# Routed expert tiles in pairs: the down product contracted as 128 rows plus two 48-row remainders

## The chip, the cores and the metric

The kernel runs on one core of one Trainium2 chip. The metric is the device time of one execution in microseconds. The time before is 397.71 us, the median of three runs (397.56 to 398.35).

## What is computed

An attention-like mixing step with a long convolution is followed by a mixture-of-experts feed-forward layer. Only the second part matters here:

```python
scores = softmax(xt @ Wg.T)                    # xt: 2048 tokens x 256, 16 experts
# 4 experts per token, out of the best 2 of 4 groups; combine holds their scores, else 0
h = silu(einsum('td,eid->eti', xt, W1)) * einsum('td,eid->eti', xt, W3)   # 176 wide
expert_out = einsum('eti,edi->etd', h, W2)
y = einsum('etd,te->td', expert_out, combine)
z = silu(xt @ Ws1.T) * (xt @ Ws3.T) @ Ws2.T    # shared experts, 352 wide
return x + y + z
```

The inner width of a routed expert, 176, is more than the 128 rows over which the array contracts in one pass.

## The kernel before

The first half of the span computes the mixing step, the router and the shared experts in 16 units of 128 tokens. Each token row is scattered to a scratch in HBM, sorted by expert, four copies of each. The **routed stage** then works through 72 tiles of 128 rows. A tile belongs to one expert; tiles 16 to 23 are **mixed**: their upper and lower 64 rows belong to two experts, and the second expert's weights ("others", 608 KB each) are loaded while tiles 5 to 14 run.

For each tile, in the order of its life:

- **gather** (SyncE, L357 to L368): one DMA of 144 KB from the scratch into one of four buffers `xg`. Gather t waits until `turn_x(t-4)` and `take(t-4)` have used that buffer. A mixed tile has two DMAs of 72 KB. The last 8 tiles go to buffers of their own (L410) and are gathered long before their use.
- **turn_x** (TensorE, L1395 to L1404): two transposes of the rows; ScalarE copies them to SBUF (`src_tr`, L547).
- **up** (TensorE, L1364 to L1385): 352 columns, contraction 256 in two matmuls. In a mixed tile each matmul is two, on the two column halves of the array (L1374 and L1377).
- **silu** (ScalarE, L553), **take** (VectorE, L1112 to L1126: the gate of each row, picked from the gathered row by the tile's expert) and **hidden** (VectorE, L1089: silu times gate times the second half of up).
- **turn_h** (TensorE, L1387 to L1393): two transposes of 88 of the 176 columns each; VectorE copies them (`copy_h`, L1096).
- **down** (TensorE, L1441 to L1459): 256 columns, contraction 88 twice (L1456), in a mixed tile on two column halves (L1448, L1451). ScalarE copies the result (`store_y`, L559).
- **place** (VectorE, L1131: the row numbers for the scatter; waits until the scatter of tile t-4 has landed) and **send** (GpSimd, L713 to L719: an indirect DMA of the tile's results to a second scratch).

Every engine's order is written out by hand. TensorE in step t: up(t), turn_x(t+1), down(t-2), turn_h(t-1). VectorE: take(t), hidden(t), copy_h(t-1), place(t). ScalarE: silu(t), src_tr(t+1), store_y(t-2). The two buffers of `up_ps`, `hid`, `ht_ps`, `hid_tr` and `dn_ps` alternate with the tile's parity.

From tile 32 on, in rounds of eight tiles, SyncE also **reads back** finished results (L392, 1024 KB for two units of tokens) and **stores** finished units (L395). In round m it issues gathers 8m to 8m+3, then the store, which waits on `finished`, then the read-back, then gathers 8m+4 to 8m+7, all on one queue. VectorE adds the read-back rows in four steps spread over the tiles of the round (L1199 to L1208); the last of them, in step j = 6, signals `finished`. The first read-back, in round 4, has no store before it. At the very start, tile 0 is turned, then `down_shared(14)` runs on TensorE, then step 0.

float32 matmuls leave two records in the trace, with a weight load each; transposes leave one.

## Time and profile before

| | |
|---|---|
| median of three runs | 397.71 us (397.56 to 398.35) |
| span of the profiled execution | 395.4 us |
| median less span | 2.3 us |
| routed stage, first up (tile 0) to last up (tile 71) | 198.60 to 382.44 us |
| TensorE busy over the span | 97% |
| mean granted TensorE clock | 0.998 |

The span runs from the first to the last instruction of the profiled execution. The profile is read per stage: a view of one stretch shows how much of it an engine was busy, and a view of instructions in order of time shows what each one waited for. Idle time of an engine that isn't the last one to be waited for costs nothing.

### The profile page before, as it was taken

Reading aid. Unit: us, or ns where it says so; the run is one execution under the profiler, and the core shown is the slowest. Engines: PE = TensorE matmul, PEld = TensorE weight load, DVE = VectorE, ACT = ScalarE, POOL = GpSimd, SP = SyncE. Lnnn points to the kernel's source line nnn. Section 1 sums busy time; section 2 is a strip of 40 time slices with the busy share of each in tenths; the row PEclk is TensorE's granted clock in tenths of the full one; section 3 lists DMA queues with packets and bytes.
Section 4 is the critical chain, followed back from the end, with each engine's and each line's share of the span. In section 5 each row is a group of like instructions: output and inputs, shape, how many; then the busy total and the mean of one; then the engine's idle time right before and its main releaser. Section 6 shows DMA issues by size and latency. Waiting matters only on the chain.

```text
span 395.4 us, 9070 instructions
## 1 busy us (share of the span) xinstructions
PE 384.7 (97%) x2146; PEld 279.3 (71%) x2147; DVE 244.1 (62%) x676; ACT 162.9 (41%) x494; POOL 180.3 (46%) x225
## 2 busy tenths in 40 slices
PE   6999999999999999999999999999999999999996
PEld 6788888888888546555667675446767777777765
DVE  3577577987988465788735344443445464646466
ACT  5347656564564362101124333333333333334431
POOL 3254323337888573565553333333333333334333
PEclk9999999999999999999999999999999999999999
DMA  7974474368879996256376873334474737362737
GB/s 248 363 254 139 163 277 144 133 206 278 309 250 335 414 419 258 96 207 223 104 215 219 321 239 107 87 95 134 127 246 136 242 115 242 115 232 103 264 97 251
DMA packets 37812, 83.09 MB, mean 210 GB/s; under 512 B 5930, under 2 KB 25870, under 8 KB 35728
## 3 DMA queue, kind: packets, MB, share of 16 engines
q1 hardware_dynamic: 31248, 64.83, 49.1%
q0 software_dynamic: 6528, 17.84, 11.6%
q8 instruction: 16, 0.26, 0.3%
q14 instruction: 20, 0.16, 0.1%
HBM read 60.21 MB, written 23.48 MB: 212 GB/s over the span
## 4 chain that ended last, share of the span: by engine, by line
PE 79%; DVE 10%; DMA 4%; issue 2%; ACT 2%; SPq 1%; DVEq 1%; POOL 0%; POOLq 0%
PE heads L1382 18%; PE bank L1456 13%; PE heads L1271 11%; PE heads L1424 7%; PE heads L1273 5%; PE bank L1437 5%; PE heads L1392 4%; PE bank L1403 4%; PE bank L1285 3%; DVE kv L734 3%; PE heads L1374 3%; DMA toep<-toep_in 2%; PE bank L1448 2%; DVE prod L763 2%; DMA y_scratch<-toep,dest_i 2%
## 5 line engine op out<-in xcount | busy, mean ns | idle before, releaser
L716 POOL DMA_INDIRECT y_scratch<-toep,dest_i x72 | 71.8, 997 | 112.0 <-DVE dest_i L1131 96.0
L1382 PE MATMUL heads<-experts,toep 128*128 x256 | 86.6, 461 | 0.6 <-DVE toep L1089 0.5
L1271 PE MATMUL heads<-toep,kv 128*128 128x256 f32 x256 | 77.9, 386 | 1.9 <-DVE kv L734 0.8
L661 POOL DMA_INDIRECT rows_scratch<-rows,slot_i x64 | 63.3, 989 | 35.4 <-issue 19.5
L1456 PE MATMUL bank<-experts,toep 88*128 x256 | 66.2, 381 | 1.6 <-DVE toep L1096 1.6
L553 ACT ACTIVATE toep<-heads 128x176 f32<-128x176 f32 x72 | 22.8, 317 | 78.1 <-PE heads L1382 67.2
L1382 PEld LDWEIGHTS heads<-experts,toep 128*128 128x128 f32 x256 | 43.7, 190 | 14.8 <-issue 1.1
L1273 PEld LDWEIGHTS heads<-toep,kv 128*128 128x128 f32 x256 | 48.7, 190 | 6.5
L763 DVE TENSOR_TENSOR prod<-heads,ctx_rep 128x1024 f32<-128x1024 f32 x32 | 39.1, 1221 | 22.3 <-PE bank L1285 19.9
L1096 DVE COPY toep<-heads 88x256 f32<-88x256 f32 x72 | 30.2, 419 | 31.1 <-PE heads L1392 31.1
L1273 PE MATMUL heads<-toep,kv 128*128 128x128 f32 x256 | 49.2, 274 | 0.0
L1456 PEld LDWEIGHTS bank<-experts,toep 88*128 88x128 f32 x256 | 43.7, 190 | 6.1 <-issue 2.3
L559 ACT ACTIVATE toep<-bank 128x256 f32<-128x256 f32 x72 | 27.6, 383 | 39.5 <-PE bank L1456 34.1
L1424 PE MATMUL heads<-xn_tr_all,ws 128*128 128x512 f32 (+1 forms) x96 | 43.5, 596 | 0.0
L1089 DVE SCALAR_TENSOR_TENSOR toep<-toep,heads 128x176 f32<-128x176 f32 x72 | 28.6, 398 | 23.2 <-ACT toep L553 18.1
L1271 PEld LDWEIGHTS heads<-toep,kv 128*128 128x128 f32 x256 | 38.8, 192 | 2.6 <-issue 1.4
L734 DVE TENSOR_TENSOR kv<-bank,ctx_tr 128x2048 f32<-128x2048 f32 x15 | 34.2, 2282 | 0.1
L1403 PEld LDWEIGHTS bank<-ident,toep 128*128 128x128 f32 x128 | 17.3, 141 | 18.8 <-issue 12.4
L1424 PEld LDWEIGHTS heads<-xn_tr_all,ws 128*128 128x128 f32 (+1 forms) x96 | 16.9, 181 | 19.0 <-issue 18.4
L547 ACT ACTIVATE toep<-bank 128x256 f32<-128x256 f32 x72 | 27.5, 382 | 5.7 <-PE bank L1403 5.5
L1392 PE MATMUL heads<-ident,toep 128*88 128x128 f32 x144 | 27.8, 275 | 0.0
L1126 DVE COPY toep<-toep 128x2 f32 x56 | 10.1, 180 | 24.1 <-issue 15.1
(240 smaller groups left out, 513.4 us busy)
## 6 DMA issues: line engine op xcount, KB each, us to landing
ctx_rep<-ctxr_in SPq DMA_DIRECT2D x16, 1024.0 KB, 5.0
experts<-experts_in SPq DMA_DIRECT2D x16, 608.0 KB
toep<-rows_scratch SPq DMA_DIRECT2D x56, 144.0 KB
prod<-y_scratch SPq DMA_DIRECT2D x5, 1024.0 KB, 5.5
rows_scratch<-pad_row SPq DMA_DIRECT2D x17, 144.0 KB, 1.8
ctx_tr<-ctxt_in SPq DMA_DIRECT2D x16, 128.0 KB
toep<-toep_in SPq DMA_DIRECT2D x4, 512.0 KB, 7.0
ctx_n<-ctx_in SPq DMA_DIRECT2D x16, 128.0 KB, 2.1
```

Of the source, the lines that this page charges most:

```text
L661: pool.indirect_dma_start(rows_d, bass.IndirectOffsetOnAxis(ap=slot_i[:, u, k:k + 1].bitcast(U32), axis=0), rows[:, u, :], None).then_inc( ...
L716: pool.indirect_dma_start(y_d, bass.IndirectOffsetOnAxis(ap=dest_i[b][:, 0:1].bitcast(U32), axis=0), y_sb[b], None, bounds_check=TOPK * TO ...
L734: nc.vector.tensor_tensor(kv[:, u % 2, :, :].rearrange("p b (g i j) -> p (b g) i j", i=C, j=C), tr_ps.rearrange("p b (g i) -> p (b g) i", ...
L763: nc.vector.tensor_tensor(prod[:, par, :, :], y_ps[par], ctx_rep[:, u % 2, par::2, :], ALU.mult).then_inc(prod_ready, 1)
L1096: nc.vector.tensor_copy(hid_tr[p], ht_ps[p]).then_inc(htr_ready, 1)
L1271: nc.tensor.matmul(y_ps[par][:, i, :], kv[:, q, 0, h * P:(h + 1) * P], toep[:, q * HH + h, :], start=True, stop=False)
L1273: last = nc.tensor.matmul(y_ps[par][:, i, P:], kv[:, q, 1, h * P:(h + 1) * P], toep[:, q * HH + h, 0:P], start=False, stop=True)
L1382: last = nc.tensor.matmul(up_ps[p], x_tr[p][:, blk, :], up_w(e, blk), start=blk == 0, stop=blk == LB - 1)
L1392: last = nc.tensor.transpose(ht_ps[p][:, c, :], hid[p][:, c * HI:(c + 1) * HI], ident[:])
L1403: last = nc.tensor.transpose(xt_ps[p][:, blk, :], src[:, blk * P:(blk + 1) * P], ident[:])
L1424: last = nc.tensor.matmul(bank[2 * (s % 2) + w][0:rows_c, :].rearrange("p (u n) -> p u n", u=GT), ws13[:, blk, w, c0:c0 + rows_c], xn_tr_a ...
L1456: last = nc.tensor.matmul(dn_ps[p], hid_tr[p][:, c, :], down_w(e, c), start=c == 0, stop=c == 1)
```

## The change

Tiles t and t+1 (t even) go as a pair. The 176 inner columns are split as 128 and 48 in place of 88 and 88.

- TensorE's step for a pair: up(t), up(t+1), turn_x(t+2), turn_x(t+3), down of the pair before, turn_h of this pair. turn_h has three transposes for both tiles: the 128 columns of each, and one block that holds both remainders (48 columns of t at 0, 48 of t+1 at 64).
- down has four products for both tiles: first the two 48-row remainders, one on partitions 0 to 47, one on 64 to 111, each into its own PSUM bank, then the two 128-row products that add to them. In mixed tiles the remainders are four, on the four quarters of the array, and the 128-row products lie on column halves.
- VectorE's step: take(t), hidden(t), take(t+1), hidden(t+1) in two instructions (48 and 128 columns), a copy of the second tile's 48 rows of W2 to the partitions from 64 on (two such copies for a mixed pair), one copy_h of 384 columns for the pair, place(t), place(t+1).
- ScalarE's step: silu twice, src_tr twice, store_y twice.
- `hid`, `ht_ps` and `hid_tr` have one buffer in place of two. The gathers, their four buffers, the loads of the others, the stores and read-backs are issued by the same code as before.
- The four adding steps of a round stand after the pairs j = 2 (step 0), j = 4 (steps 1 and 2) and j = 6 (step 3).
- Before tile 0's up, both tile 0 and tile 1 are turned.

The core of the diff:

```diff
+            def routed_pair(t, b, before):            # ScalarE
+                silu(t, 0)
+                silu(t + 1, 1)
+                if not (isinstance(t, int) and t == LIVE - 2):
+                    src_tr(t + 2, 0)
+                    src_tr(t + 3, 1)
+                if not (isinstance(t, int) and t == 0):
+                    for i in range(2):
+                        store_y(t - 2 + i, i, (b - 2) % DEPTH + i, before if b >= 2 else before - 1)
...
-                nc.vector.scalar_tensor_tensor(hid[p], act1[p], picked[:, b, 0:1], up_ps[p][:, INTER:],
-                                               ALU.mult, ALU.mult).then_inc(hid_ready, 1)
+                if p == 0:
+                    nc.vector.scalar_tensor_tensor(hid[:, 0:INTER], act1[p], picked[:, b, 0:1], up_ps[p][:, INTER:],
+                                                   ALU.mult, ALU.mult).then_inc(hid_ready, 1)
+                else:
+                    nc.vector.scalar_tensor_tensor(hid_rest[:, HALF:HALF + REM], act1[p][:, P:], picked[:, b, 0:1],
+                                                   up_ps[p][:, INTER + P:], ALU.mult, ALU.mult)
+                    nc.vector.scalar_tensor_tensor(hid_main[p], act1[p][:, 0:P], picked[:, b, 0:1],
+                                                   up_ps[p][:, INTER:INTER + P], ALU.mult, ALU.mult).then_inc(hid_ready, 1)
...
+            def rest_of_w2(t, e, first):
+                if not (isinstance(t, int) and t < 2):
+                    dve.wait_ge(rest_done, pair_of(t))
...
+            def routed_pair(t, b, before):            # VectorE
+                first = take(t, b, before)
+                hidden(t, 0, b)
...
+                e = take(t + 1, b + 1, before)
+                hidden(t + 1, 1, b + 1)
...
+                rest_of_w2(t, e, first if is_mixed(t) else None)
+                copy_h(pair_of(t))
                 place(t, b, before)
+                place(t + 1, b + 1, before)
...
-                    if pair is not None and 3 <= j <= 6:
-                        add_pair(pair, u0, j - 3)
+                    if pair is not None and j >= 2:
+                        for step in ((0,), (1, 2), (3,))[j // 2 - 1]:
+                            add_pair(pair, u0, step)
...
+            def turn_h(t):
+                m = pair_of(t)
+                pe.wait_ge(hid_ready, t + 2)
+                if not (isinstance(t, int) and t < 2):
+                    pe.wait_ge(htr_ready, m)
+                for p in range(2):
+                    nc.tensor.transpose(ht_ps[:, p, :], hid_main[p], ident[:])
+                nc.tensor.transpose(ht_ps[:, 2, :], hid_rest, ident[:]).then_inc(ht_done, 1)
...
+                nc.tensor.matmul(dn_ps[0], hid_tr[rest[0], 2, :], rest_w(e[0]), start=True, stop=False)
+                nc.tensor.matmul(dn_ps[1], hid_tr[rest[1], 2, :], w2_rest[rest[1], :], start=True, stop=False
+                                 ).then_inc(rest_done, 1)
+                for i in range(2):
+                    nc.tensor.matmul(dn_ps[i], hid_tr[:, i, :], down_w(e[i]), start=False, stop=True).then_inc(dn_done, 1)
...
             turn_x(0, 0, 0, 0)
+            turn_x(1, 1, 1, 0)
             down_shared(UNITS - 2)
...
+            def routed_pair(t, b, before):            # TensorE
+                up(t, 0, b)
+                up(t + 1, 1, b + 1)
+                if not (isinstance(t, int) and t == LIVE - 2):
+                    for i in range(2):
+                        turn_x(t + 2 + i, i, (b + 2) % DEPTH + i, before + 1 if b == DEPTH - 2 else before)
...
+                    down(t - 2, (b - 2) % DEPTH)
+                turn_h(t)
```

## Rows read from the trace of the kernel before

**Rows 1.** Busy times by stretch: us, then each engine, clock, DMA share, GB/s.

```profile
198.60:235.40 36.80, 35.23 (x165) 25.49 (x164) 16.47 (x67) 13.06 (x40) 15.64 (x16) 1.00 0.77 254
305.25:365.01 59.76, 59.76 (x290) 44.32 (x289) 32.64 (x108) 23.82 (x73) 23.61 (x24) 1.00 0.51 172
```

**Rows 2.** Order of time, TensorE, one plain tile: start us, us, instruction, count.

```profile
342.60 1.35 PE L1382 MATMUL heads<-experts,toep 128*128 x4
343.79 0.38 PE L1403 MATMUL bank<-ident,toep 128*128 128x128 f32 x2
344.00 1.03 PE L1456 MATMUL bank<-experts,toep 88*128 x4
344.87 0.38 PE L1392 MATMUL heads<-ident,toep 128*88 128x128 f32 x2
345.09 0.46 PE L1382 MATMUL heads<-experts,toep 128*128 x1
```

**Rows 3.** Order of time, TensorE, a tile with its down on column halves.

```profile
268.31 0.38 PE L1403 MATMUL bank<-ident,toep 128*128 128x128 f32 x2
268.62 0.43 PE L1448 MATMUL bank<-experts,toep 88*64 x1
268.63 0.43 PE L1451 MATMUL bank<-rows,toep 88*64 88x256 f32 x1
...
269.64 0.42 PE L1392 MATMUL heads<-ident,toep 128*88 128x128 f32 x2
269.89 0.46 PE L1382 MATMUL heads<-experts,toep 128*128 x1
```

**Rows 4.** Order of time, TensorE, two mixed tiles: where each up begins.

```profile
258.31 0.51 PE L1374 MATMUL heads<-experts,toep 128*64 x1
...
261.38 0.51 PE L1374 MATMUL heads<-experts,toep 128*64 x1
```

**Rows 5.** Order of time, VectorE, beside Rows 2: copy, place, add, take, hidden.

```profile
342.80 0.42 DVE L1096 COPY toep<-heads 88x256 f32<-88x256 f32 x1 [0.56 <-PE heads L1392]
343.14 0.14 DVE L1131 CAST dest_i<-toep 128x1 int32<-128x1 f32 x1
343.20 0.68 DVE L1208 TENSOR_TENSOR resid<-resid,prod 128x512 f32 x1
343.95 0.20 DVE L1126 COPY toep<-toep 128x2 f32 x1
344.34 0.40 DVE L1089 SCALAR_TENSOR_TENSOR toep<-toep,heads 128x176 f32<-128x176 f32 x1 [0.19 <-ACT toep L553]
```

**Rows 6.** Order of time, SyncE's queue: gather, store, read-back, gather.

```profile
345.02 0.33 SPq L368 DMA_DIRECT2D toep<-rows_scratch  x1
346.38 0.41 SPq L395 DMA_DIRECT2D out<-resid  x1
347.12 0.39 SPq L392 DMA_DIRECT2D prod<-y_scratch  x1
348.46 4.28 SPq L368 DMA_DIRECT2D toep<-rows_scratch  x3
```

**Rows 7.** DMA issues by kind: count, KB each, median us from issue to landing.

```profile
prod<-y_scratch SPq DMA_DIRECT2D x5, 1024.0 KB, 5.5
kv<-experts_in SPq DMA_DIRECT2D x3, 608.0 KB, 6.1
rows<-rows_scratch SPq DMA_DIRECT2D x8, 144.0 KB, 2.5
```

**Rows 8.** Order of time, SyncE's queue, while the others are loaded.

```profile
217.24 0.33 SPq L368 DMA_DIRECT2D toep<-rows_scratch  x1
218.35 0.33 SPq L377 DMA_DIRECT2D kv<-experts_in  x1
```

**Rows 9.** Order of time, SyncE's queue, the first read-back.

```profile
287.18 0.40 SPq L392 DMA_DIRECT2D prod<-y_scratch  x1
```

**Rows 10.** Order of time, weight loads: turn_x that waited for its gather.

```profile
293.41 0.22 PEld L1403 LDWEIGHTS bank<-ident,toep 128*128 128x128 f32 x2 [0.32 <-DMA toep<-rows_scratch]
```

157 lines of the change are left out of this document (73 added, 84 removed).

## The prediction

> **What bounds the kernel now.** I read the routed stage alone, first by stretch. From tile 40 to tile 64 TensorE is busy for all of its 59.76 us VectorE for 32.64 and the weight loads, which run beside the matmuls, for 44.32, at a granted clock of 1.00 [rows 1]. So a microsecond taken from TensorE there is a microsecond of the kernel, unless something else becomes the last to arrive. From tile 0 to tile 14 the same view shows 36.80 us. Fourteen tiles at the steady step of 2.49 us [rows 2] would take 34.86, so 1.94 us are waits, in the stretch in which the others are loaded (DMA share 0.77 against 0.51). The steady step itself, in order of time, is up 1.19, turn_x 0.21, down 0.87, turn_h 0.22 [rows 2], without a hole. The three things to read next are what a change of the array's tiling costs, how early VectorE frees a gather buffer, and what lies ahead of a gather on SyncE's queue.
>
> **The change on TensorE.** A pair takes 2 x 2.49 = 4.98 us now. After it: two ups 2.38, four transposes of turn_x 0.43, two 128-row products 0.87 (as long as now: the time goes with the 256 columns), three transposes 0.33, and the remainders. Each remainder is two passes of about 0.22 (0.87 for four), so both cost 0.43 if they run at once and 0.87 one after the other. No row shows two products on two row halves; the nearest is two on two column halves, which start 0.01 us apart and take 1.02 us for what takes 0.87 whole [rows 3]. I take "at once", and keep the other end as a rival.
>
> The remainders also change the tiling of the array twice per pair. Its price is bounded by the same rows: turn_x to down is 0.31 in place of 0.21, down to turn_h 1.02 in place of 0.87, turn_h to up 0.25 in place of 0.22 [rows 2, 3], together 0.28 for a change there and back. The lower end is 0, if row halves need no emptying of the array, the upper one twice 0.28; I take 0.28 because the products on both sides are the same. A pair is then 2.38 + 0.43 + 0.43 + 0.87 + 0.33 + 0.28 = 4.72, a gain of 0.26.
>
> The Trainium skill (TensorEngine Tiling (Array Packing), Key Properties) states that changing the tiling mode drains the engine, which speaks against this change; the trace agrees for column halves, with the 0.28 above, and shows none for rows.
>
> Mixed pairs change the tiling less often than now. Two mixed tiles with mixed downs take 6.14 now (a step of 3.07 [rows 4]); so up's change costs 3.07 - 2.49 - 0.28 = 0.30. After: 4.44 for the work, 0.30 once for the ups, three changes for remainders, main products and back at 0.14 each: 5.16, a gain of 0.98. Three blocks gain that, the one with only its ups mixed about 0.56, the one with only its downs 0.68: 4.2 together.
>
> Sum on TensorE: 28 plain pairs that still count before the end x 0.26 = 7.3, mixed 4.2, the first pair about 0.5: **-12.0 us**. What hides the rest: the second hidden in two instructions (0.40 as one [rows 5], I take 0.65), the copy of W2 rows (0.3 to 0.4, by the copy of 0.42 there) and the copy of 384 columns (0.55 by the same row) all lie on VectorE, which has 27 us free in the 59.76 [rows 1]. Of the new waits, turn_h's on both hiddens (behind it stands the next pair's up) is met: hidden(t+1) ends about 3.9 us into the pair, turn_h stands at 4.4. The W2 copy's on the remainders of the pair before (behind it, copy_h) is met at about 3.5, before the copy comes up. The single buffers of hid, ht_ps and hid_tr are freed by work that TensorE has done before the step that refills them. Uncovered, each would cost its own length per pair.
>
> **What is late next: the gathers.** Let a pair start at 0. The copy for the pair before starts at 0.20 and is longer by 0.13, its two places follow, take(t) is 0.8 after a place [rows 5]: at 1.6. Hidden(t) follows 0.39 later, at 2.0, and take(t+1), which stands behind it on VectorE, at 2.8. A gather is issued 1.07 after the take that frees its buffer [rows 5, 6]: gather t+4 at 2.7, gather t+5 at 3.9. Its rows are wanted by turn_x(t+5), at 4.72 + 2.38 + 0.2 = 7.3 (t+4: 7.1). Landing takes 2.5 in quiet [rows 7]: 6.4, in time by 0.9. Today take(t) and the turn are nearly three steps apart, so this margin is what the pairing spends. Where a large transfer stands ahead on the queue, it isn't enough:
>
> *Others.* Between two gathers stands a load of 608 KB, 1.1 us after the gather before it [rows 8], landing 6.1 later [rows 7]; a gather behind such a transfer lands some 0.4 to 0.7 after it, as the first read-back shows (issued at 287.18, 5.5 to land, turn_x released at 293.41) [rows 7, 9, 10]. The load ahead of gather t+5 leaves at 3.8, so the gather lands at 3.8 + 6.1 + 0.4 = 10.3, 3.0 late. The stall lengthens that pair, which gives the next gathers as much more time, so it comes about every second pair: in the five pairs of that stretch two full ones, plus 0.5 where the list work on VectorE delays take(4). 6.4 us against 1.94 now: **+4.5** (2.5 to 6).
>
> *Mixed gathers.* Two DMAs per tile, 1.1 to 1.3 apart on SyncE: the second of t+5 leaves at about 6.0 and lands at 8.5, against 7.5; by the same alternation some 2.5 us over the four pairs: **+2.5** (1 to 4).
>
> *Read-backs.* The last adding step now follows the pair j = 6. With S the start of the next pair it ends at S + 0.20 + 0.47 + 0.2 + 0.68 = S + 1.55. SyncE's store waits for that and holds what is queued behind it: the read-back 0.74 after the store [rows 6], at S + 2.4, which lands 5.5 later [rows 7] at S + 7.9, the gather behind it at S + 8.3. It is wanted at S + 7.1, and its neighbour at S + 7.3 lands later still. Stall 1.2 to 1.9, I take 1.5, in each of rounds 5 to 7: **+4.5**. Round 4 has no store to wait for and stalls now by 0.32 [rows 10]; it gets about the same: **+1.2**. In the last round the tiles are gathered long before: nothing.
>
> *Start and end.* Tile 1 is turned before `down_shared(14)`; its gather is issued 1.1 after that of tile 0 (spacing in [rows 8]) and nothing stands between: **+0.9**. The last down waits for a copy of 384 columns after turn_h: **+0.4**.
>
> Sum: -12.0 + 4.5 + 2.5 + 4.5 + 1.2 + 0.9 + 0.4 = +2.0 on a span of 395.4, so 397.4; the median lies 2.3 above the span now and I keep that: 399.7.
>
> **Rivals.** *The change there and back is cheap* (on the other side: not slower). Some 20 pairs don't stall, and there the change of tiling costs directly; where a pair stalls, a faster one only waits longer. At 0 in place of 0.28 that is -5.6: 394. It decides from 0.10 less per pair on: below 0.18 the kernel is no longer slower. For it: the remainders and the main products use the same columns; against it, column halves are no cheaper.
>
> *The gathers come in time.* Then 397.7 - 12.0 + 1.3 + part of the waits for the others: 387 to 392. For it: today even gathers behind a read-back cost 0.32 at most [rows 10]. Against it: that margin is three steps of a tile, and a pair leaves 0.9.
>
> *The remainders run one after the other.* The change then does not do what it says: a pair takes 5.16, 0.18 more than now. Over the 23 pairs that don't stall by more, that is 0.43 x 23 = 9.9 above the forecast: 410. The Trainium skill (TensorE: Matmul & The Clock Gate, Part 3) gives measured speedups for row tiles, 3.07 for four; by it they run at once. No run here shows it.
>
> **How the numbers follow.** Forecast 399.7 (397 to 403): 0.58. Cheap change of tiling (392.5 to 397): 0.17. Gathers in time (386 to 392.5): 0.12. One after the other (406 to 413): 0.13. The range 392.5 to 405.5 holds the first two and leaves 0.2 out, beyond its bounds on either side. About 0.2% (0.8 us) is what a measurement of this kernel can tell from no change: faster takes the two cheap cases but a part of one, 0.26; within it 0.16; slower 0.58.
>
> **What would show it.** In order of time on TensorE: the two remainders start within 0.02 us of each other (right) or 0.43 apart; from the fourth transpose of turn_x to turn_h's first 1.6 us; plain pairs of 4.72 in tiles 26 to 34 and 48 to 52. Weight loads of turn_x released by gathers, with 1 to 3 us idle before them, twice in tiles 6 to 16 and once in each round from 4 to 7. SyncE's store waiting for the adding step in rounds 5 to 7. It is wrong if the stalls don't appear, if VectorE instead of a gather ends the waits, or if a pair is above 4.9 without a stall. A stall of 3 us could also lower the granted clock, which stayed at 1.00 with the waits of today [rows 1]; I give that no price.

## The result and the profile after

The changed kernel takes 408.92 us (median of 4 runs, 406.74 to 410.19); the kernel before, run beside it, 397.63 (396.79 to 398.35). The ratio is 1.0273, with a 95% interval of 1.0248 to 1.0298: slower by 2.7%. The profiled run took 410.19 us with a span of 408.4, 13.0 more than before.

Where the 13.0 us came from is read by stretch, between the starts of the first up product of a tile (rows of each stretch in order of time on TensorE; the difference is after less before):

| stretch | before, us | after, us | difference | forecast by the prediction's terms |
|---|---|---|---|---|
| start of tile 0 | 198.60 | 200.48 | +1.9 | +0.9 |
| tiles 0 to 14 | 36.80 | 42.32 | +5.5 | +2.4 |
| tiles 14 to 28 | 39.47 | 37.43 | -2.0 | -2.2 |
| tiles 28 to 70 | 105.08 | 111.84 | +6.8 | +0.2 |
| from tile 70 to the end | 15.45 | 16.37 | +0.9 | +0.4 |

The ends of the span are read to a tenth of a microsecond. By stretch the prediction's terms add up to +1.7 (its own +2.0 counts one plain pair less). Two stretches carry the error. The windows that answer to [rows 1] (us, then busy time and instructions of each engine, granted clock, DMA share, GB/s) show the same:

```profile
200.48:242.80 42.32, 36.03 (x161) 23.48 (x159) 19.34 (x74) 13.59 (x40) 15.27 (x16) 0.98 0.70 225
313.27:376.41 63.14, 60.59 (x277) 39.21 (x277) 34.69 (x118) 23.52 (x72) 23.84 (x25) 1.00 0.49 161
```

From tile 40 to 64 TensorE was busy for all of 59.76 us; now it has 2.55 us of holes in 63.14. Three lines of the list of waits from 200 to 392 us (engine, line, what ended the wait: total us, times, longest) name the holes:

```profile
PE bank L1440 <- DMA toep<-rows_scratch: 5.1, 4, 2.5
PE heads L1417 <- issue: 3.6, 5, 0.9
PE heads L1429 <- DVE toep L1103: 2.8, 5, 1.2
```

L1440 is turn_x, waiting for a gather; L1429 is turn_h, waiting for the second hidden product on VectorE (L1103), which the prediction had declared met; and L1417 is the up product, idle for 3.6 us with nothing that the profile can name.

A plain pair that waits for nothing, in order of time on TensorE (start, us, instruction, count), answers to [rows 2]:

```profile
365.98 2.53 PE L1417 MATMUL heads<-experts,toep 128*128 x8
368.35 0.60 PE L1440 MATMUL bank<-ident,toep 128*128 128x128 f32 x4
368.88 0.48 PE L1503 MATMUL bank<-experts,toep 48*128 x1
368.89 0.48 PE L1504 MATMUL bank<-toep 48*128 48x256 f32 x1
369.20 0.38 PE L1503 MATMUL bank<-experts,toep 48*128 x1
369.21 0.38 PE L1504 MATMUL bank<-toep 48*128 48x256 f32 x1
369.51 1.13 PE L1507 MATMUL bank<-experts,toep 128*128 x4
370.48 0.38 PE L1429 MATMUL heads<-ident,toep 128*128 128x128 f32 x2
370.70 0.27 PE L1430 MATMUL heads<-ident,toep 128*128 128x128 f32 x1
370.81 0.46 PE L1417 MATMUL heads<-experts,toep 128*128 x1
```

The two remainders (L1503, L1504) start 0.01 us apart: they do run at once. The pair takes 370.81 - 365.98 = 4.83 us, 0.15 less than two tiles of before, where 0.26 was forecast. The four transposes should be over at 368.35 + 0.43 = 368.78; the remainders start 0.10 later and the first main pass 0.63 after them, and the main passes (the 128-row products) take 0.97 to turn_h in place of 0.87.

One pair of a read-back round, that of tile 54, on VectorE and TensorE (in brackets the idle time before the instruction and what ended it; "..." stands for rows left out):

```profile
350.58 0.68 DVE L1234 TENSOR_TENSOR prod<-prod 128x512 f32<-128x512 f32 x1
351.29 0.69 DVE L1237 TENSOR_TENSOR prod<-prod 128x512 f32<-128x512 f32 x1
352.19 0.17 DVE L1150 COPY toep<-toep 128x2 f32 x1 [0.21 <-issue]
...
353.51 0.17 DVE L1150 COPY toep<-toep 128x2 f32 x1 [0.63 <-issue]
...
353.98 0.34 DVE L1103 SCALAR_TENSOR_TENSOR toep<-toep,heads 128x128 f32<-128x128 f32 x1
354.47 0.43 PE L1429 MATMUL heads<-ident,toep 128*128 128x128 f32 x2
355.90 2.63 PE L1417 MATMUL heads<-experts,toep 128*128 x8 [0.90 <-issue]
```

Two adding steps in a row (L1234, L1237) put the pair's first take (L1150) at 352.19, 2.54 us after the pair's start at 349.65; the second hidden product ends at 354.32, 4.67 into the pair instead of 3.75 to 3.85; turn_h starts late at 354.47. The first up product of the next pair then starts only 1.58 us behind that hidden product, although turn_h's three passes need 0.33. This pair takes 6.25 us. The same happens in the pairs of tiles 38, 46 and 62 (6.48, 6.24, 5.60).

The time from the hidden product to the next up product is lost even where turn_h doesn't wait. The end of the pair of tile 50, whose hidden product is over at 343.35:

```profile
343.01 0.34 DVE L1103 SCALAR_TENSOR_TENSOR toep<-toep,heads 128x128 f32<-128x128 f32 x1
344.21 0.38 PE L1429 MATMUL heads<-ident,toep 128*128 128x128 f32 x2
344.73 0.56 PE L1417 MATMUL heads<-experts,toep 128*128 x1
```

Here turn_h stands where the passes before it end, and the next up product still starts 0.52 us behind it, 1.38 behind the hidden product. Over all pairs of this kernel and of the seven runs that keep turn_h at the end of the pair (1 to 5, 7 and 8), the next up product never started sooner behind the second hidden product than 0.71 us where TensorE's steps are written out one by one (from tile 60 on, for instance), 0.91 within an iteration of its loop, and 1.32 behind the end of an iteration (in this kernel behind the pairs of tiles 30, 34, 38 and so on to 54). By the program, the transposes, the end of the loop and two loads of the expert's register stand between turn_h's wait and that up product.

In the stretch of the others, TensorE and SyncE's queue:

```profile
216.81 0.33 SPq L373 DMA_DIRECT2D toep<-rows_scratch  x1
217.95 0.33 SPq L382 DMA_DIRECT2D ws<-experts_in  x1
218.73 0.38 PE L1440 MATMUL bank<-ident,toep 128*128 128x128 f32 x2
221.64 0.44 PE L1440 MATMUL bank<-ident,toep 128*128 128x128 f32 x2 [2.53 <-DMA toep<-rows_scratch]
```

Tile 9's gather (issued at 216.81, landed at 221.60, with a load of an expert on either side of it) holds its turn_x for 2.53 us; tile 15's holds it for 1.66 more. These are the forecast stalls. The pair of tile 10 lost 0.95 us in another way: VectorE's place waited 1.20 and 0.52 us for scatters, so its takes and its second hidden product came late.

### The profile page after: what moved, and what is told of

It reads as the page before. It is cut to its first block, busy times and chain, and to the rows that moved or that the text cites. A ratio compares the mean times of both kernels' runs of the same rounds, so it can differ in the third digit from the quotient of the medians.

```text
span 408.4 us, 8971 instructions
## 1 busy us (share of the span) xinstructions
PE 384.0 (94%) x2110; PEld 265.4 (65%) x2111; DVE 254.5 (62%) x717; ACT 162.2 (40%) x494; POOL 181.5 (44%) x225
## 4 chain that ended last, share of the span: by engine, by line
PE 61%; DVE 15%; DMA 9%; issue 7%; SPq 3%; ACT 2%; DVEq 1%; POOL 1%; POOLq 0%; ACTq 0%
PE heads L1417 12%; PE heads L1303 9%; PE heads L1461 6%; PE bank L1507 5%; PE heads L1305 5%; DVE kv L742 4%; DMA toep<-rows_scratch 3%; PE bank L1440 3%; PE bank L1503 3%; PE bank L1474 3%; PE bank L1317 3%; DMA y_scratch<-toep,dest_i 3%; PE heads L1409 2%; DVE prod L771 2%; PE heads L1429 2%
## 5 line engine op out<-in xcount | busy, mean ns | idle before, releaser
L1417 PE MATMUL heads<-experts,toep 128*128 x256 | 83.1, 468 | 4.1 <-issue 3.6
L669 POOL DMA_INDIRECT rows_scratch<-rows,slot_i x64 | 63.1, 986 | 37.4 <-issue 19.2
L1417 PEld LDWEIGHTS heads<-experts,toep 128*128 128x128 f32 x256 | 46.7, 192 | 27.7 <-issue 7.3
L564 ACT ACTIVATE toep<-bank 128x256 f32<-128x256 f32 x72 | 26.8, 384 | 34.1 <-PE bank L1507 30.2
L1507 PE MATMUL bank<-experts,toep 128*128 x128 | 36.9, 412 | 0.0
L1120 DVE COPY toep<-heads 128x384 f32<-128x384 f32 x36 | 20.1, 558 | 26.8 <-PE heads L1430 26.8
L1507 PEld LDWEIGHTS bank<-experts,toep 128*128 128x128 f32 x128 | 22.0, 191 | 12.4 <-issue 10.6
L552 ACT ACTIVATE toep<-bank 128x256 f32<-128x256 f32 x72 | 24.7, 382 | 12.1 <-PE bank L1440 11.7
L1440 PE MATMUL bank<-ident,toep 128*128 128x128 f32 x128 | 21.3, 279 | 6.1 <-DMA toep<-rows_scratch 5.2
L1440 PEld LDWEIGHTS bank<-ident,toep 128*128 128x128 f32 x128 | 15.3, 141 | 17.9 <-DMA toep<-rows_scratch 8.1
L1098 DVE SCALAR_TENSOR_TENSOR toep<-toep,heads 128x176 f32<-128x176 f32 x36 | 14.3, 397 | 18.8 <-ACT toep L558 16.9
L473 ACT ACTIVATE spread<-resid 128x256 f32<-128x256 f32 x32 | 13.2, 411 | 27.6 <-POOL resid L660 22.1
```

The lines of the kernel that those rows point to most:

```text
L552: nc.scalar.activation(x_tr[p], xt_ps[p], ACT.Copy).then_inc(xtr_ready, 1)
L564: nc.scalar.activation(y_sb[b], dn_ps[p], ACT.Copy).then_inc(y_ready, 1)
L669: pool.indirect_dma_start(rows_d, bass.IndirectOffsetOnAxis(ap=slot_i[:, u, k:k + 1].bitcast(U32), axis=0), rows[:, u, :], None).then_inc( ...
L1417: last = nc.tensor.matmul(up_ps[p], x_tr[p][:, blk, :], up_w(e, blk), start=blk == 0, stop=blk == LB - 1)
L1440: last = nc.tensor.transpose(xt_ps[p][:, blk, :], src[:, blk * P:(blk + 1) * P], ident[:])
L1507: nc.tensor.matmul(dn_ps[i], hid_tr[:, i, :], down_w(e[i]), start=False, stop=True).then_inc(dn_done, 1)
```

## Experiments

Lengths of pairs are differences of the starts of the first up product, read in order of time on TensorE. A table of stretches for all of them (us; the last column is the ratio to the kernel before with its interval):

| kernel | start of tile 0 | tiles 0 to 28 | 28 to 70 | 70 to end | median | ratio |
|---|---|---|---|---|---|---|
| before | 198.60 | 76.27 | 105.08 | 15.45 | 397.6 | 1 |
| after | 200.48 | 79.75 | 111.84 | 16.37 | 408.92 | 1.0273 [1.0248, 1.0298] |
| adding step moved | 199.26 | 78.29 | 110.44 | 17.41 | 406.86 | 1.0259 [1.0190, 1.0328] |
| takes first | 199.85 | 77.26 | 111.81 | 17.18 | 405.94 | 1.0203 [1.0172, 1.0234] |
| remainders on the whole array | 200.15 | 76.72 | 111.05 | 17.08 | 407.44 | 1.0261 [1.0196, 1.0325] |
| loads cut | 200.06 | 74.91 | 112.17 | 17.46 | 404.85 | 1.0152 [1.0090, 1.0214] |
| eight tiles per iteration | 199.81 | 78.75 | 110.66 | 16.28 | 405.88 | 1.0181 [1.0141, 1.0222] |
| turn_h one pair on | 200.28 | 77.77 | 114.33 | 17.02 | 412.64 | 1.0396 [1.0352, 1.0440] |
| lists later | 200.44 | 82.56 | 111.17 | 17.33 | 411.46 | 1.0322 [1.0285, 1.0360] |
| no remainders (one run) | 199.69 | 75.64 | 107.30 | 15.77 | 400.18 | |
| turn_h one pair on, gathers first | 199.32 | 80.42 | 113.61 | 17.45 | 412.04 | 1.0360 [1.0315, 1.0405] |
| and five moves | 198.58 | 73.89 | 104.07 | 17.76 | 398.95 | 1.0037 [1.0010, 1.0064] |
| and two more | 198.94 | 71.46 | 110.62 | 18.28 | 398.53 | 1.0016 [0.9992, 1.0039] |
| and the adds a pair later | 198.51 | 71.45 | 104.82 | 17.72 | 396.84 | 0.9988 [0.9973, 1.0004] |

Runs of one kernel with pairs differ by 2 to 3 us around their median, those of the kernel before by 1, so a verdict here rests on a stretch or on pairs of the profile and only then on the time. A stretch varies as well: runs 1 and 5 leave everything up to tile 28 as it was, and tile 0 starts at 199.26 and 199.81 in them instead of 200.48, tiles 0 to 28 take 78.29 and 78.75 us instead of 79.75, and the pair of tile 6 takes 9.33 and 6.63 instead of 7.67. The lengths of the pairs in the read-back rounds, for the kernels that changed them:

| pair of tile | 34 | 36 | 38 | 40 | 42 | 44 | 46 | 48 | 50 | 52 | 54 | 56 | 58 | 60 | 62 |
|---|---|---|---|---|---|---|---|---|---|---|---|---|---|---|---|
| after | 6.94 | 4.92 | 6.48 | 5.17 | 5.13 | 4.92 | 6.24 | 4.92 | 5.08 | 4.92 | 6.25 | 4.92 | 5.15 | 4.83 | 5.60 |
| adding step moved | 6.91 | 4.92 | 5.64 | 5.79 | 5.11 | 4.92 | 5.39 | 5.09 | 6.12 | 4.95 | 5.68 | 4.97 | 5.70 | 4.83 | 4.94 |
| eight tiles per iteration | 7.09 | 4.99 | 5.78 | 5.06 | 5.75 | 4.91 | 5.52 | 5.02 | 5.95 | 4.83 | 5.61 | 5.02 | 5.51 | 4.83 | 5.59 |
| turn_h one pair on | 6.81 | 4.83 | 4.87 | 4.93 | 6.30 | 4.83 | 4.83 | 4.83 | 7.49 | 5.61 | 4.83 | 4.83 | 8.05 | 5.89 | 4.83 |
| adds a pair later (last) | 4.83 | 6.04 | 4.99 | 4.93 | 4.83 | 6.77 | 4.83 | 4.83 | 4.83 | 4.83 | 4.83 | 4.83 | 4.83 | 4.83 | 4.83 |

**1. One adding step moved into its pair.**

```diff
                 rest_of_w2(t, e, first if is_mixed(t) else None)
+                if under is not None:
+                    under()
                 copy_h(pair_of(t))
...
+                    under = None
+                    if pair is not None and j == 4:
+                        under = lambda: add_pair(pair, u0, 1)
...
-                        for step in ((0,), (1, 2), (3,))[j // 2 - 1]:
+                        for step in ((0,), (2,), (3,))[j // 2 - 1]:
```

> Only the place of one adding step is changed: step 1 of the read-back rounds goes from behind the pair at j=4, where it stood in a row with step 2, into that pair, between the copy of the second remainder and the copy of the turned hidden rows, where VectorE waits 0.96 us for TensorE anyway. Theory A (VectorE is late after two adding steps of 0.68 in a row, so the pair at j=6 waits at its turn_h and then once more, 0.9 us, at the first up product of the next iteration of TensorE's loop): the pairs that begin with tiles 38, 46, 54 and 62 fall from 6.48, 6.24, 6.25 and 5.60 us to about 4.92, together 4.9 us, and the time from 408.9 to about 404.0. Theory B (these pairs wait for a gather or a read-back): they stay, 408.9.

The waits at turn_h in the pairs of tiles 38, 46, 54 and 62 are gone, as theory A says, and those pairs fall to 5.64, 5.39, 5.68 and 4.94 us. They don't fall to 4.92, because the idle time of the next up product stays without any wait of turn_h, and the pairs of tiles 40, 50 and 58 grow to 5.79, 6.12 and 5.70: tiles 40 to 64 take 63.5 us, 63.1 without the move, and the time is 406.86, not the 404.0 expected. So VectorE's lateness was real, but taking it away only uncovered the next limit: ahead of the takes of tiles 40 and 50 VectorE's place now waits 0.46 and 0.76 us for a scatter.

**2. Both takes ahead of both hidden products.**

```diff
                 first = take(t, b, before)
+                e = take(t + 1, b + 1, before)
                 hidden(t, 0, b)
                 if isinstance(t, int) and t == 0:
                     add_z(UNITS - 2)
-                e = take(t + 1, b + 1, before)
```

> Both takes of a pair stand ahead of both hidden products, nothing else is changed. In the kernel after the change VectorE is idle for 0.5 to 0.9 us ahead of the second take, behind the first hidden product, with nothing to wait for. Theory A (this idle time is the take's own register work, and the chain take, hidden, take, hidden is what TensorE's turn_h waits for, where anything comes before it): the second hidden product comes about 0.7 us sooner and the second take about 1 us sooner, so the waits at turn_h go (pairs 38, 46, 54, 62: 4.9 us together, and of pair 4's 1.2 some 0.7), and the gather of tile t+5 is issued 0.5 to 1 us sooner, which takes some 2 us from the gather waits of tiles 6 to 20: about 401 to 402. Theory B (VectorE's order doesn't matter, the waits are those of transfers): 408 to 409.

Tiles 28 to 70 stay at 111.81. VectorE in the pair that answers to the one shown above:

```profile
349.15 0.17 DVE L1150 COPY toep<-toep 128x2 f32 x1 [0.20 <-issue]
350.07 0.17 DVE L1150 COPY toep<-toep 128x2 f32 x1 [0.76 <-issue]
...
350.88 0.34 DVE L1103 SCALAR_TENSOR_TENSOR toep<-toep,heads 128x128 f32<-128x128 f32 x1
```

The idle time ahead of the second take moved with it (0.63 us there, 0.76 here). So it belongs to the take and is not time that this order could fill; by the program a load of a register stands there, which the trace doesn't show. The chain from the first take's start to the end of the second hidden product was 354.32 - 352.19 = 2.13 and is 351.22 - 349.15 = 2.07. Theory A falls on that point. In the profile, 2.5 us less in tiles 0 to 28 go with the smaller median; 1.0 to 1.5 of that is what this stretch varies by without any edit.

**3. The remainders on the whole array.** Each plain sum takes in the other tile's remainder as well.

```diff
-                nc.tensor.matmul(dn_ps[0], hid_tr[rest[0], 2, :], rest_w(e[0]), start=True, stop=False)
-                nc.tensor.matmul(dn_ps[1], hid_tr[rest[1], 2, :], w2_rest[rest[1], :], start=True, stop=False
-                                 ).then_inc(rest_done, 1)
+                for i in range(2):
+                    last = nc.tensor.matmul(dn_ps[i], hid_tr[:, 2, :], rest_w(e[i]), start=True, stop=False)
+                last.then_inc(rest_done, 1)
```

> The remainders of a plain pair's down product are contracted over the whole array instead of on its two row halves: the two products use all 128 rows of the turned remainder of both tiles and of the expert's remainder rows, so each sum takes in the other tile's remainder as well; the mixed pairs are as they were. There is no tiling change left in a plain pair. Theory A (the row halves save what their two passes at once measure, 0.63 us from the first remainder to the first main pass instead of four passes of 0.22 us, less 0.10 for the change of tiling ahead): the unstalled plain pair goes from 4.83 to 4.97 us, as much as two tiles of before (4.98), and the time to about 411 to 412. Theory B (the row halves save nothing, all is eaten by the tiling change): pair 4.83, 408.9. Theory C (the price recorded in the prediction, 0.28 for there and back against 0.43 saved, with 4.72 reached where nothing else delays): pair 4.98 and over 412.

```profile
362.80 2.53 PE L1417 MATMUL heads<-experts,toep 128*128 x8
365.17 0.60 PE L1440 MATMUL bank<-ident,toep 128*128 128x128 f32 x4
365.61 1.03 PE L1504 MATMUL bank<-experts,toep 128*128 x4
366.47 1.03 PE L1507 MATMUL bank<-experts,toep 128*128 x4
367.34 0.38 PE L1429 MATMUL heads<-ident,toep 128*128 128x128 f32 x2
367.67 2.53 PE L1417 MATMUL heads<-experts,toep 128*128 x8
```

The unstalled pair is 367.67 - 362.80 = 4.87 us with four whole passes in place of two on halves: the row halves save 0.03 to 0.04 us a pair. Theory B is nearest. What the pair does save, 4.98 - 4.87 = 0.11, is the fourth transpose of turn_h. The price of the halves follows from the two traces: 365.61 to 366.47 is 0.86 for four whole passes; on halves it is 0.10 ahead (0.53 from 368.35 to 368.88, in place of 0.44), 0.63 for the passes and 0.10 behind the main passes, 0.83 together. In this run the weight loads of the remainders and of the main passes start 0.11 and 0.21 us ahead of their products (365.50 and 366.26); with the halves they start together with them (368.88 and 369.51).

**4. The loads of the others cut to 64 columns.** The mixed tiles are computed with what lay in that memory.

```diff
-                sp.dma_start(other_mem[g], experts_d[:, bass.ds(e, 1), :].rearrange("p a n -> p (a n)")).then_inc(other_in[g], 16)
+                sp.dma_start(other_mem[g][:, 0:64], experts_d[:, bass.ds(e, 1), 0:64].rearrange("p a n -> p (a n)")).then_inc(other_in[g], 16)
```

> The eight loads of the experts of the mixed tiles are cut to 64 of their 1,216 or so columns, so the mixed tiles are computed with what lies in that memory; all waits and the order of the queue stay. Theory A (in the first sixteen tiles the gathers are late since they share the DMA engines with these loads): the waits of turn_x at tiles 6, 12 and 14 (2.5, 0.2 and 1.7 us) and most of those at 16 and 20 (0.5 and 0.4) go, with what the clock lost after them (about 1 us): tile 16 starts some 5 to 6 us sooner, about 403 in all; pair 4's wait at turn_h, 1.2, stays, being VectorE's. Theory B (the gathers are late because of when they are issued, two tiles in a row behind one pair's takes): the same waits remain, within 1 us, 408.

```profile
218.28 0.69 PE L1440 MATMUL bank<-ident,toep 128*128 128x128 f32 x4
```

Tile 9's gather, issued at 216.37, lands in 2.12 us instead of 4.79 and turn_x of the pair of tile 6 has no hole: 5.02 us instead of 7.67. Tiles 0 to 16 take 43.14 us instead of 47.93 (45.65 and 46.70 in runs 1 and 5, which don't touch them). Theory A holds: 4.8 of the 5 to 6 us against the changed kernel, 2.5 and 3.6 against those two runs. One wait of 1.80 us is left, in the pair of tile 8, for gather 11, which still took 4.07 us.

**5. TensorE's loop with eight tiles per iteration**, so that its ends stand behind the pairs of tiles 34, 42, 50 and 58; the other engines' loops are as they were.

```diff
-            with eng.Fori(until // DEPTH, static // DEPTH) as it:
-                for b in range(0, DEPTH, 2):
-                    step(it * DEPTH + b, b, it)
+            with eng.Fori(2, 6) as it:
+                for b in range(0, 2 * DEPTH, 2):
+                    step(it * 8 + 12 + b, b % DEPTH, it * 2 + 3 + b // DEPTH)
```

> TensorE's loop over the plain tiles from 28 on takes eight tiles in one iteration instead of four, so its loop end stands behind the pairs of tiles 34, 42, 50 and 58 only. In the kernel after the change, and in the two runs that moved an adding step and the takes, the first up product behind a loop end starts 1.37 to 1.59 us behind the end of the second hidden product, the one that turn_h waited for, with or without a visible wait of turn_h. Theory A (the sequencer of TensorE is held by turn_h's wait, and what it has to do between that wait and the first product of the next iteration takes longer than the 0.3 us of turn_h's passes, so the loop end shows): behind pairs 38, 46 and 54 the idle 0.9 us at the next up product goes, those pairs fall from 6.48, 6.24 and 6.25 to about 5.5, and the pairs 34, 42, 50 and 58 stay as they are (6.9, 5.13, 5.08, 5.15): tiles 28 to 70 from 111.8 to about 109, the time 408.9 to about 406. Theory B (the up product waits for data): the idle time stays behind 38, 46 and 54, 408.9.

```profile
352.41 0.34 DVE L1108 SCALAR_TENSOR_TENSOR toep<-toep,heads 128x128 f32<-128x128 f32 x1
352.89 0.43 PE L1434 MATMUL heads<-ident,toep 128*128 128x128 f32 x2
...
353.70 0.56 PE L1422 MATMUL heads<-experts,toep 128*128 x1 [0.26 <-issue]
```

Where no loop end follows, the late turn_h is followed by the next up product after 0.81 us (352.89 to 353.70) instead of 1.43 (354.47 to 355.90); the idle time is 0.26 instead of 0.90 and the pairs fall to 5.78, 5.52 and 5.61 (5.5 expected). From the end of the hidden product at 352.75 it is 0.95 us, in place of 1.58. Theory A holds. The pairs of tiles 42, 50 and 58, where the loop ends still stand, grew by 0.4 to 0.9 with waits for gathers, so tiles 28 to 70 gained 1.2 and not 2.8.

**6. turn_h one pair on.** It stands behind the next pair's first up product, and VectorE's copy behind the next pair's first take.

```diff
                 up(t, 0, b)
+                if not (isinstance(t, int) and t == 0):
+                    turn_h(t - 2)
                 up(t + 1, 1, b + 1)
...
                     down(t - 2, (b - 2) % DEPTH)
-                turn_h(t)
```

> A pair's turn_h stands behind the first up product of the next pair instead of at the end of its own, and VectorE copies the turned rows between the next pair's first take and first hidden product; nothing else is changed, the down product stays where it is. Theory A (what the change lost is the slack of turn_h: in the kernel before it waited for the hidden rows of the tile before, ready some 2 us earlier, in the kernel after for the last hidden product of the same pair, ready 0.5 us earlier where nothing disturbs VectorE): no wait at turn_h, no idle time at loop ends, the pairs from 28 on take 4.83 to 4.92 us unless a gather waits, tiles 28 to 70 go from 111.8 to 102 to 104 us, pair 4 from 6.5 to about 5.3, and the time from 408.9 to 397 to 400. Theory B (VectorE itself is at its limit, with 4.2 us of work and register loads in a pair, so that it only moves its delay): pairs of 5.1 and more, 404 to 408. The waits for gathers in tiles 6 to 16 stay in both.

All waits at turn_h and all holes at loop ends are gone, and the plain pairs in which nothing waits take 4.83 to 4.94, pair 4 among them (4.83; 6.52 before). But the time rose, above all because three pairs now wait for a gather and for VectorE. TensorE and SyncE's queue in the first of them:

```profile
311.10 0.42 SPq L400 DMA_DIRECT2D out<-resid  x1
311.85 0.39 SPq L397 DMA_DIRECT2D prod<-y_scratch  x1
313.19 7.56 SPq L373 DMA_DIRECT2D toep<-rows_scratch  x4
317.78 0.44 PE L1442 MATMUL bank<-ident,toep 128*128 128x128 f32 x2 [0.95 <-DMA toep<-rows_scratch]
```

Store, read-back and gather 44 stand in that order; the gather, issued at 313.19, lands at 317.73 behind the read-back (317.36), 4.54 us instead of 2.1. This is the stall that the prediction forecast for the rounds. The pairs of tiles 42, 50 and 58 are 1.5, 2.7 and 3.2 us longer than 4.83, of which turn_x waits 0.95, 0.69 and 1.50 us for the gather. The rest has two other sources. VectorE's place waits 2.94, 2.73 and 3.89 us for a scatter in these pairs, and in the last two the down product then waits 0.66 and 0.59 for the copy behind it. And behind these waits the granted clock falls, here after those of tile 50 (us, busy times, clock, DMA share, GB/s):

```profile
340.00:342.20 2.20, 2.20 (x8) 1.54 (x7) 1.87 (x8) 0.38 (x1) 0.00 (x0) 0.59 0.25 67
```

The main passes then take 1.87 us in place of 0.97 (340.36 to 342.23), and the next up product is longer too, in the pair of tile 52 (5.61). In the changed kernel as it stands the stall is hidden, since VectorE's lateness had held the start of the round back, but not the read-back: it left 1.6 us after the start of the pair of tile 40 there (314.86 against 313.27) and 2.8 after it here (311.85 against 309.04). Neither theory of the run foresaw it: the mechanism of theory A is right and its time wrong.

**7. The list work of VectorE later** (behind tiles 18 and 20 instead of 2 and 4).

```diff
-                    if isinstance(m, int) and m == 0 and j in (2, 4):
+                    if isinstance(m, int) and m == 2 and j in (2, 4):
```

> The two stretches of VectorE's list work that stood behind the pairs of tiles 2 and 4 stand behind those of tiles 18 and 20, among the mixed tiles; nothing else is changed. Theory A (this work, 2.2 us behind pair 2, makes the takes of tiles 4 to 6 late, and with them the second hidden product of pair 4 and the gathers of tiles 8 and 9, which are issued only behind a take): pair 4 falls from 6.52 to 4.8 to 5.1 us, pair 6 from 7.67 to 5.5 to 6.5, tile 8 starts 2.5 to 3.5 us sooner after tile 0, and the pairs of tiles 18 and 20 get at most 1 us longer each: 406 to 408. Theory B (tile 6 waits for a gather that the loads of the experts delay, whenever it is issued): only pair 4's 1.2 us go, and come back as a longer wait at tile 6: 408 to 409.

```profile
221.46 0.44 PE L1440 MATMUL bank<-ident,toep 128*128 128x128 f32 x2 [3.39 <-DMA toep<-rows_scratch]
```

Pair 4 fell to 5.15 and pair 6 rose to 9.78: its turn_x was released at 221.46, as in the changed kernel (221.64). Theory B holds, though the time lies above what either theory gave. Tile 8 starts 24.2 us after tile 0, 23.5 in the changed kernel (24.9 and 22.4 in runs 1 and 5), where theory A wanted 2.5 to 3.5 less. These gathers come at a fixed time: SyncE's queue waits for the last scattered rows until 212.9 in both, and behind that stand the loads. The moved work cost 2.1 and 1.7 us in the pairs of tiles 20 and 22, more than the 1 expected.

**8. No remainders at all** in the plain pairs (each sum lacks 48 of 176 terms).

```diff
-                nc.tensor.matmul(dn_ps[0], hid_tr[rest[0], 2, :], rest_w(e[0]), start=True, stop=False)
-                nc.tensor.matmul(dn_ps[1], hid_tr[rest[1], 2, :], w2_rest[rest[1], :], start=True, stop=False
-                                 ).then_inc(rest_done, 1)
                 for i in range(2):
-                    nc.tensor.matmul(dn_ps[i], hid_tr[:, i, :], down_w(e[i]), start=False, stop=True).then_inc(dn_done, 1)
+                    last = nc.tensor.matmul(dn_ps[i], hid_tr[:, i, :], down_w(e[i]), start=True, stop=True)
+                    last.then_inc(dn_done, 1)
```

> One look: the plain pairs leave out both remainder products, so each sum lacks 48 of its 176 terms; the mixed pairs are as they were. It prices the remainders on the row halves, with all that they cost in tiling changes: the pair that waits for nothing is 4.83 us with them and was 4.86 with the remainders over the whole array. Theory A (two passes at once at 0.22 us each, and 0.2 to 0.3 us for the change of tiling there and back): 4.83 - 0.43 - 0.28 = 4.1 us. Theory B (the passes on row halves take 0.31 us each and the change costs 0.2 us ahead and behind together): about 4.0. Theory C (the tiling change is free and the remainders take 0.43): 4.4.

```profile
206.49 0.60 PE L1440 MATMUL bank<-ident,toep 128*128 128x128 f32 x4
206.93 1.03 PE L1504 MATMUL bank<-experts,toep 128*128 x4
207.79 0.38 PE L1429 MATMUL heads<-ident,toep 128*128 128x128 f32 x2
```

From turn_x to turn_h it is 1.30 us (206.49 to 207.79, without a hole) where it was 2.13 (368.35 to 370.48), so the remainders on row halves cost 0.83 us with all their changes of tiling, what run 3 gave. By the length of the pair that is 4.00, theory B, but no pair got there: those of 4.17 to 4.5 us still wait at turn_h or for the next up product, so VectorE's chain sets them. With 0.83 us less on TensorE none of the pairs that took 4.83 falls by more than 0.66, and tiles 28 to 70 took 107.30 us, still more than before the change.

**9. Gathers of a round ahead of its store and read-back**, on top of run 6.

```diff
+                gathers(m, DEPTH, DEPTH + 2)
                 store(m - 5, m * 2 - 10, 2)
                 read_back(m - 4, m * 2 - 8, 2, back, back_in, sends)
-                gathers(m, DEPTH, 2 * DEPTH)
+                gathers(m, DEPTH + 2, 2 * DEPTH)
```

> As the run with turn_h behind the next pair's first up product, and in each read-back round SP issues the gathers of the round's fifth and sixth tile ahead of the store and the read-back instead of behind them. In that earlier run the waits at turn_h and at the loop ends were gone and all undisturbed pairs took 4.83 us, but the pairs of tiles 42, 50 and 58 had become 6.30, 7.49 and 8.05 us, with waits of turn_x for a gather that landed 4.2 to 4.5 us after its issue behind a 1024 KB read-back, instead of 2.1. Theory A (the read-back round is the second limit, hidden in the kernel after the change by VectorE's lateness; the gather is late since it stands behind the store's wait and the read-back): the three pairs fall to 4.83 to 5.0, with the disturbed ones behind them; tiles 40 to 64 go from 67.2 us to 58 to 59, the time from 412.6 to about 404. Theory B (the transfers of a round are too much wherever the gathers stand): the wait moves to the gathers of the seventh tile or to VectorE's adds, tiles 40 to 64 stay above 63, 409 or more.

Theory B holds: the pairs of tiles 42, 50 and 58 all fall to 4.83, and the pairs of tiles 44, 52 and 60 rise to 7.17, 6.31 and 6.64. Tiles 40 to 64 take 64.8 us, not 58 to 59. VectorE's place of tile 42 then waits 2.84 us, until 324.60, for a scatter that runs beside the read-back (319.04 to 324.60), and holds the first adding step, the next take and the copy behind it.

**10. Five more moves**, on top of run 9 (the diff shows the first): turn_x of the second tile behind down, the first read-back behind gathers 36 and 37, the late gathers behind gather 39, place one pair back, tile 1 turned behind tile 0's up.

```diff
+                if more:
+                    turn_x(t + 2, 0, (b + 2) % DEPTH, before + 1 if b == DEPTH - 2 else before)
...
                     down(t - 2, (b - 2) % DEPTH)
+                if more:
+                    turn_x(t + 3, 1, (b + 2) % DEPTH + 1, before + 1 if b == DEPTH - 2 else before)
```

> As the run before in this list, with five more moves of the same kind and no change of the arithmetic: the turning of a pair's second tile stands behind the down product (1.6 us later, so its gather has that much more), the first read-back stands behind the gathers of tiles 36 to 37, the late gathers behind those of 38 and 39, VectorE's place of a tile goes one pair back so that its wait for a scatter no longer holds the takes and the copy, and tile 1 is turned behind the first up product of tile 0. Theory A (all of what the change lost against its 4.83 us a pair are waits that these moves take away): the waits of turn_x at tiles 6, 12 and 14 shrink by 1 to 1.6 us each, pair 34 from 6.8 to under 5.5, tiles 28 to 70 take 102 to 104 us (105.1 in the kernel before), tile 0 starts 1 us sooner, and the time is 395 to 399, the same as the kernel before within a per cent. Theory B (the transfers in the first sixteen tiles set the pace whatever waits for them): tiles 0 to 16 stay at 46 to 48 us (41.9 before), and the time at 400 to 403.

The median is 398.95, at the edge of theory A's 395 to 399. Tile 0 starts at 198.58, as before the change; the pair of tile 6 takes 7.73 (10.35 in run 6), those of 12 and 14 fall to 5.06 and 5.02 (6.38 and 6.62 there), tiles 28 to 70 take 104.07. The profiled run, 396.09, is the fastest of the twelve, so its stretches flatter the kernel; the same holds for run 12 (394.26), while that of run 11 (401.06) is among the slowest.

**11. Loads behind the gathers, and the tail** (the expectation numbers the first pair two too high: it is that of tile 6).

```diff
-            others_at = {5: (0,), 7: (1,), 8: (2,), 9: (3,), 10: (4,), 11: (5,), 13: (6,), 14: (7,)}
+            others_at = {5: (0,), 9: (1,), 11: (2,), 12: (3,), 13: (4,), 14: (5,), 15: (6,), 16: (7,)}
```

> As the run with all five moves, and two more: the loads of the mixed tiles' experts after the first stand behind the gathers of tiles 9, 11, 12, 13, 14, 15 and 16 instead of 7, 8, 9, 10, 11, 13 and 14, and at the end VectorE copies the last pair's turned rows and gives its places ahead of the last adding step instead of behind it. In that run tiles 28 to 70 took 104 us less the loss at two read-back rounds, and what was left were waits of 0.9 and 1.2 us for gathers in the pair of tile 8 (7.73 us) and an end of 17.8 us behind the start of tile 70 (15.5 in the kernel before). Theory A (the gathers of tiles 8 to 11 are late because 608 KB loads stand between them): pair 8 falls to 4.9 to 6, the end gets 0.3 to 0.6 us shorter, the time goes from 398.95 to 396 to 397.5. Theory B (they are late because of the wait for the last scattered rows, which ends at the same moment in all runs, and the transfers that follow): pair 8 stays above 7, 398 to 399.

The pair of tile 6 falls from 7.73 to 4.83 and tiles 0 to 28 take 71.46 us, 4.8 less than in the kernel before. So theory A holds for these gathers: the loads between them made them late. The time, 398.53, is nevertheless theory B's. The end did not get shorter (18.28), and the pairs of tiles 36, 52 and 60 (the next expectation numbers the last two 54 and 62) took 8.91, 6.64 and 6.46 us; in them VectorE's first adding step waited 3.85, 3.21 and 2.98 us for the read-back.

**12. The adding steps a pair later.**

```diff
-                        for step in ((0,), (1, 2), (3,))[j // 2 - 1]:
+                        for step in ((), (0, 1), (2, 3))[j // 2 - 1]:
```

> As the run with seven moves, and the adding steps of a read-back round one pair later: none behind the pair at j=2, steps 0 and 1 behind that at j=4, steps 2 and 3 behind that at j=6. In that run tiles 0 to 16 had no wait for a gather left, and what was lost from tile 28 on, against 4.83 us a pair, were 8.91, 6.64 and 6.46 us at the pairs of tiles 36, 54 and 62, where VectorE waited 3.9 and 3.2 us with its first adding step for a read-back that took 6.1 to 7.0 us, and held the next take and copy. Theory A (the first adding step is the last thing that the late read-back holds): those three pairs fall to 4.83 to 5.2, tiles 28 to 70 take 101.5 to 103 us (105.1 in the kernel before), and the time goes from 398.5 to 391 to 394, less than the kernel before. Theory B (two adding steps of 0.68 us behind each of two pairs make VectorE late again): pairs behind j=4 and j=6 of 5.2 to 5.6, 395 to 398.

```profile
198.51:227.81 29.30, 28.74 (x136) 19.36 (x135) 15.50 (x65) 10.07 (x32) 13.74 (x14) 1.00 0.73 238
269.96:374.78 104.82, 102.21 (x485) 67.76 (x484) 57.26 (x206) 39.46 (x126) 41.35 (x42) 1.00 0.55 176
```

Tiles 0 to 12 (the first window) run with half a microsecond of holes, and from tile 46 on every pair takes 4.83. Theory A holds where the adds were the cause: the pairs of tiles 52 and 60 are 4.83. Its time of 391 to 394 didn't come. Two stalls are left, 6.04 at tile 36 and 6.77 at tile 44, where turn_x waits 1.68 us for a gather behind the read-back. The median is 396.84; the ratio 0.9988, whose interval holds 1. With these moves the changed kernel takes as long as the kernel before: tiles 0 to 28 are 4.8 us shorter, but the end has grown by 2.3 us, in which TensorE waits 2.34 us for the last read-back. That was not followed further, and none of the moves was tried on the kernel before, so how much of the gain they would give without the change stays open.

## Why the prediction was wrong

The direction was right and most of the mechanisms named for it are in the traces; the size, +2.0 on the span forecast, +13.0 measured, was not. The step that failed is "turn_h's wait is met": some 9 us were lost behind late hidden products in seven pairs, where the prediction had nothing. By its steps:

- *The remainders run at once* (right: 0.01 us apart; the rival of 410 falls, though its time was near).
- *The pair of 4.72* was mis-sized by 0.11: it takes 4.83. The prediction priced two passes on row halves as two whole passes, 0.43, and the tiling change at 0.28 from column halves [rows 3]. Measured: the two passes on halves take 0.63, 0.31 or 0.32 each and not 0.22; the change costs 0.10 ahead and 0.10 behind. 28 pairs x 0.15 is 4.2 us, not 7.3. The Trainium skill (TensorEngine Tiling (Array Packing), Key Properties) says that a change of tiling mode drains the engine; the trace agrees, with 0.20 for row halves. The Trainium skill (TensorEngine Tiling (Array Packing), Theoretical Speedup) allows a speedup of up to 2 where a dimension is at most 64; in these traces 0.86 whole against 0.83 on halves is 1.04. The 0.83 lies inside the bounds that were kept (0.43 to 0.99); what they hid is that the nearest row for an operation at half a height was one at half a width, with the same 256 columns.
- *turn_h's wait is met* was the step that failed most. The hidden product of an undisturbed pair came as forecast (done 3.4 to 3.85 us into it, 3.9 forecast), and turn_h stood behind it (at 4.50). But the margin was taken to the wrong instruction: the next up product, which the prediction names as what stands behind turn_h, needs 0.91 us after the hidden product within TensorE's loop and 1.32 to 1.59 behind its end, and the forecast's own 4.72 - 3.9 left 0.82. So pairs ahead of a loop end had no slack even with VectorE on time (5.08 for that of tile 50). The step also left out the two adding steps of 0.68 in a row behind the pair at j = 4, though the change's diff puts them there, and it took the list work of 2.2 us behind tile 2 only as a delay of a gather. And it priced a late turn_h at its own lateness. Behind a late turn_h stands the end of TensorE's loop: 0.9 us more (run 5 takes 0.64 of it away by moving the loop end). Rounds 4 to 7 lost 1.65 + 1.41 + 1.42 + 0.77 = 5.3 us by this, the pairs of tiles 4, 10 and 68 1.7, 0.95 and 1.1.
- *Read-backs, +4.5 and +1.2*: mechanism right, place taken by the line above. The pairs of tiles 42, 50 and 58 were 0.2 to 0.3 us longer, those of 42 and 50 at the loop end and not for a gather; with VectorE's lateness removed (run 6), turn_x waited 0.95, 0.69 and 1.50 us in them, and waits of VectorE and the clock came on top. Round 4 lost 2.1, of which 0.65 is the wait for its gather and 0.9 the loop end behind it.
- *Others, +4.5 (2.5 to 6)*: right in kind, and at the lower end of its range in size. The term is 6.4 us of waits (its parts, two of 3.0 and 0.5, make 6.5) less the 1.94 of before; turn_x waits 2.53 + 0.22 + 1.66 = 4.4 us, 2.5 more than before. What came on top are VectorE's lateness in the pairs of tiles 4 and 10 and the clock.
- *Mixed gathers, +2.5*: 0.9, below its own lower bound of 1. Ahead of turn_x stand holes of 0.53 and 0.37, which the view puts down to nothing that it knows.
- *The clock*, which was mentioned and given no price: after the 1.66 us wait in the pair of tile 12, the work from 240.51 to 245.86 takes 5.35 us where an undisturbed pair needs 3.67 (369.51 to 373.18). That is 1.7 us.
- *Start and end* cost 1.9 and 0.9 instead of 0.9 and 0.4; with the same program up to tile 28, runs 1 and 5 have 0.7 and 1.2 for the start.

From tile 28 to 70 the terms are: 21 pairs x 0.11 = 2.3 less gained, 5.3 at the ends of rounds, 1.1 at tile 68 (VectorE again, 0.59 us of wait), 0.4 more in round 4 than the 0.5 of before and the 1.2 forecast, 0.3 at tile 40, 0.75 in eight pairs of 4.92 to 4.95 (the two up products behind a loop end take 2.63 instead of 2.53), less 3.6 for the read-back stalls that stayed hidden: 6.6 against the 6.5 that were missing. The prediction's list of what would make it wrong held the right item, "if VectorE instead of a gather ends the waits", and gave it no rival and no chance.

Open is why the next up product comes 1.58 or 1.59 us behind the hidden product at some loop ends of the changed kernel and 1.37 at others, and how much of the spread of the pair kernels' times is the clock.

## What to carry to other kernels

Working on two tiles at once halves the number of steps and also the slack that each wait had: list every wait with its margin in the new order, and set against the smallest margin the longest thing that ever stands ahead of its producer, not the usual one. Take the margin to the instruction where the engine would next run dry, and not to the wait itself: here that was the up product behind turn_h. When two limits lie close, the first one hides the second, so a stall that doesn't appear where it was forecast is not yet disproved. And before an engine's array is split, compare the split with the unsplit work in the same order of loops: here the pairing gave what was gained, and the halves 0.03 us.
